# Mamba, time-warped cross-attention and 64 experts on one core: GpSimd scatters an expert's rows ahead of the gather for the expert four places on

## The reference

```
logits = einsum('te,ex->tx', x, gate)            # 4096 tokens, 64 experts
weights, selected = top_k(logits, 2); weights = softmax(weights)
sorted_x = x[token_idx]                          # 8192 rows, grouped by expert
h0, h1 = ragged_dot(sorted_x, w0), ragged_dot(sorted_x, w1)   # 256 -> 512, float32
out_sorted = ragged_dot(silu(h0) * h1, wo)                    # 512 -> 256
out[t] = sum over its 2 experts of weight * out_sorted[row]
x = x + out
```

## Time and profile before

| | |
|---|---|
| median of 3 runs | 1307.4 us (1305.8 to 1307.7) |
| the profiled execution's own time | 1307.59 us |
| its span, first to last instruction | 1305.8 us |
| mean granted TensorE clock | 0.888 |
| busy: TensorE, DVE, GpSimd, ACT | 1036.5, 927.7, 695.1, 580.2 us |
| gathers (L2221) in the profile | 93, mean 0.997 us of GpSimd |
| scatters (L2228) in the profile | 95, mean 1.575 us of GpSimd |
| the experts' stretch | about 837 to 1262 us |

### The profile page before, as it was taken

One profiled execution on the slowest core, in us unless ns is written; L12 is line 12 of the kernel. 1 busy time (PEld: TensorE's weight loads), 2 busy tenths in 40 slices (PEclk: granted clock), 3 DMA queues, 4 the chain that ended last, 5 costly groups with the idle time before them and its releaser, 6 DMA issues. The chain is left out here.

```text
span 1305.8 us, 21090 instructions
## 1 busy us (share of the span) xinstructions
PE 1036.5 (79%) x6867; PEld 924.2 (71%) x6867; DVE 927.7 (71%) x2072; ACT 580.2 (44%) x1286; POOL 695.1 (53%) x609
## 2 busy tenths in 40 slices
PE   5767888787878768477746788799999999999970
PEld 4666767686767757466511576599999999999960
DVE  6999999999999996688798599433333333333348
ACT  3768787878778764344340454121221222222210
POOL 4886868788888870200000554346556565655620
PEclk8889989999999999555578899599999999999985
DMA  8644555464646551122203244499999999999939
GB/s 241 191 142 143 162 164 176 135 203 140 190 150 199 158 168 42 26 41 49 41 1 129 89 149 151 167 291 277 267 271 281 292 288 303 295 306 298 278 105 351
DMA packets 177597, 239.82 MB, mean 184 GB/s; under 512 B 33778, under 2 KB 104486, under 8 KB 176848
## 3 DMA queue, kind: packets, MB, share of 16 engines
q1 hardware_dynamic: 153968, 215.06, 52.1%
q0 software_dynamic: 17184, 18.97, 7.0%
q10 hardware_dynamic: 6336, 4.44, 1.1%
HBM read 203.01 MB, written 31.19 MB: 179 GB/s over the span
## 5 line engine op out<-in xcount | busy, mean ns | idle before, releaser
L1010 PE MATMUL st_y_ps<-ident,st_hc 128*128 128x128 f32 x2048 | 273.6, 292 | 113.3 <-DVE st_hc L529 113.2
L1010 PEld LDWEIGHTS st_y_ps<-ident,st_hc 128*128 128x128 f32 x2048 | 255.4, 203 | 135.6 <-DVE st_hc L529 134.7
L412 POOL TENSOR_TENSOR st_u<-st_dx,codes 128x1024 f32<-128x1024 f32 x127 | 296.4, 2361 | 39.2 <-DVE st_h L521 31.4
L521 DVE TENSOR_TENSOR_SCAN st_h<-st_da,st_u 128x512 f32<-128x512 f32 x256 | 297.6, 1203 | 0.2 <-POOL st_u L412 0.2
L2288 PE MATMUL mo_h<-mo_xt,w 128*128 128x128 f32 (+17 forms) x2048 | 282.1, 289 | 2.0 <-DVE mo_xt L2411 2.0
L2288 PEld LDWEIGHTS mo_h<-mo_xt,w 128*128 128x128 f32 x2048 | 271.6, 193 | 6.6 <-issue 2.7
L2417 DVE TENSOR_TENSOR mo_inter<-mo_silu,mo_h 128x128 f32<-128x128 f32 (+17 forms) x256 | 77.8, 304 | 246.2 <-ACT mo_silu L2370 204.3
L2228 POOL DMA_INDIRECT outs<-mo_o,choice x95 | 149.6, 1575 | 149.2 <-DVE mo_o L2428 130.3
L2370 ACT ACTIVATE mo_silu<-mo_h 128x128 f32<-128x128 f32 (+17 forms) x256 | 74.4, 291 | 286.6 <-PE mo_h L2288 198.5
L748 ACT ACTIVATE st_da<-st_delta,st_a_neg 128x510 f32<-128x510 f32 x256 | 172.1, 685 | 58.6 <-DVE st_h L521 54.1
L529 DVE TENSOR_TENSOR st_hc<-st_h,st_cps 128x1024 f32<-128x1024 f32 x128 | 152.5, 1192 | 0.0
(11 more groups left out here) (394 smaller groups left out, 1472.9 us busy)
## 6 DMA issues: line engine op xcount, KB each, us to landing
codes<-bc SPq DMA_DIRECT2D x256, 256.0 KB, 3.7
w<-in_L_ffn_w_dram SPq DMA_DIRECT2D x128, 512.0 KB
wo<-in_L_ffn_wo_dram SPq DMA_DIRECT2D x64, 512.0 KB
outs<-ex_zero SPq DMA_DIRECT2D x16, 512.0 KB, 3.2
co_got<-outs SPq DMA_DIRECT2D x16, 512.0 KB, 6.0
wave<-dist SPq DMA_DIRECT2D x16, 274.0 KB
x<-in_x_dram SPq DMA_DIRECT2D x8, 512.0 KB, 9.4
st_cx<-in_ctx_dram SPq DMA_DIRECT2D x8, 512.0 KB, 4.0
```

The costliest lines, as they stand in the source:

```text
L412: nc.gpsimd.tensor_tensor(u_sb[k % URING][:, :, :], dx[p % 2][:, :, :], over_chunks(b_sb[k % BRING]), ALU.mult).then_inc(u_ok, 1)
L521: nc.vector.tensor_tensor_scan(h_sb[k % HRING][:, dh, :], da_ps[dh][:, :], u_sb[k % URING][:, dh, :], 0.0, ALU.mult, ALU.add).then_inc(h_o ...
L1010: m = nc.tensor.matmul(y_ps[t // 2][:, t % 2, dh * P:(dh + 1) * P], hc_sb[k % RING][:, dh, t * P:(t + 1) * P], K.ident[:, :], start=False, ...
```

## The change

In GpSimd's loop over places, the scatter of place k is called ahead of the gather for place k+4, and no longer behind it (and behind the copy and the late gather, at place 59).

```
             for k in range(RANKS):
+                scatter(k)
                 if k + XR < RANKS:
                     gather(k + XR)
                 if k + XR == RANKS:
...
                                                  ).then_inc(x_in[LAST], 16)
-                scatter(k)
             n = late_count(pool)
```

## The result

| | before | after |
|---|---|---|
| median | 1307.38 us (6 runs, 1305.8 to 1308.04) | 1311.51 us (6 runs, 1309.84 to 1312.11) |
| ratio | | 1.0028 (1.0018 to 1.0039) |
| the profiled execution: time, span | 1307.59, 1305.8 us | 1312.11, 1310.4 us |

What follows compares the result with a forecast made beforehand. The prediction took TensorE's matmuls to bound the experts' stretch. With nothing added and nothing exposed, it forecast an unchanged median of 1307.4 us (chance 0.82), range 1304.5 to 1311 us.

Steps and rivals of the forecast that it cites:

- What bounds the kernel: Experts' stretch, 860 to 1240 us: TensorE busy 380.00 of 380 us, so a GpSimd change can only lengthen it.
- What moves: GpSimd's queue: same instructions and durations; even gathers go out 9.1 us later, odd gathers 4.4, odd scatters 1.2.
- The even gathers' room: Last issue of an even gather to TensorE's turn: 8.7 us at place 50, smallest 8.5 at place 62; cost nothing.
- The odd scatters' 1.2 us: Odd scatters start 1.2 us later; DVE needs their output buffer four places on, so hidden, over 9 us to spare.
- The first rival, late even gathers: Even gathers land after TensorE's turn, stalling every second one, 15 stalls: 12 us slower, 1319; chance 0.11.
- small form: Late even gathers at only the crowded first few places, up to 1 us each: 1 to 5 us, 1308 to 1312.
- The second, collision with the weights: Even gathers push weight loads back on the DMA engines, 0.5 us each, 15 us if exposed 30 times: 1322; chance 0.02.
- Scatters get ahead: Results seem to leave earlier; at most place 4's gather frees the first weight loads, 2.5 us, 1305; chance 0.05.
- What would show it: Signs in the changed profile: GpSimd's new order, TensorE busy 380.0 of 380, no weight-load wait for a DMA into gathered rows.

Runs made afterwards that it cites:

- e1: The changed kernel, with each odd place's scatter also waiting for the fourth up-product of the wide place behind it: 1308.95 us, ratio 1.0007.
- e5: The kernel before in its own order, with each odd place's scatter also waiting for DVE's second product of the next wide place: 1306.62 us, ratio 0.9995.
- e9: The changed kernel with a GpSimd memset of 0.54 us behind every gather: 1307.33 us, ratio 0.9998.
- e6: The changed kernel without the weight loads of places 4 to 62, which reuse the first four places' weights: 1311.83 us, ratio 1.0040.
- e4: The kernel before with the scatter moved ahead of the gather at even places alone: 1335.76 us, ratio 1.0206.
- e8: e4 with plain scatters, which write their rows without the add: 1357.82 us, ratio 1.0385.
- e11: The kernel before, in its own order, with plain scatters that write without the add: 1332.93 us, ratio 1.0190.
- e7: e4 without the weight loads of places 4 to 62, which reuse the first four places' weights: 1326.69 us, ratio 1.0153.
- e3: The kernel before with the scatter moved ahead of the gather at odd places alone: 1307.59 us, ratio 0.9997.
- e10: e4 with a GpSimd memset of 0.54 us behind every gather: 1307.42 us, ratio 0.9997.
- e12: The kernel before with plain scatters and a GpSimd memset of 0.33 us behind every gather and scatter: 1314.15 us, ratio 1.0043.

## Why the prediction was wrong

- **What bounds the kernel** held: TensorE's matmuls, at a clock of 1.00, and no DMA that they wait for. What I took from it didn't hold: that with TensorE at 380 of 380 us there is only the DMA to ask about. ACT and DVE stand in a chain between the up-products and the down-products of the same place, and for small rooms that chain has 0.4 us of slack.
- **What moves** held to 0.1 us: two scatters, two gathers, scatter, gather. In place 58 the scatter starts 3.28 us behind the place's beginning by the forecast's pattern and 3.30 us in the trace.
- **The even gathers' room** held. No turn waited for a gather. The last one went out 8.96 us ahead of the turn of place 62, for 8.5 forecast:

```profile
1241.39 0.91 POOL L2221 DMA_INDIRECT mo_xg<-xn,table  x1 [0.30 <-issue]
...
1250.35 0.59 PE L2274 MATMUL mo_xt_ps<-ident,mo_xg 128*128 128x128 f32 x4
```

The landing time in it was too short: the trace's records of landings, incomplete as they are, have the last one of an even gather 6.1 us after its issue in the median, 7.1 at place 10 and 8.2 at place 6, where the forecast took 5.4 (place 50: 5.5). That left 2.4 us ahead of the turn at the least.

- **The step that failed** is the one on "The odd scatters' 1.2 us", answered with "Hidden, over 9 us to spare", with nothing in the sum for it. GpSimd's durations did stay the same (scatters 149.7 us in all, for 149.6), but I asked only who waits for the scatter's rows. Moved behind two gathers, it is the third indirect DMA in 2.6 us, and in that row TensorE's signal to ACT is held for 0.28 to 0.67 us in each wide place from 32 to 60: 3.8 us instead of nothing. e1 (scatter out of the row: no loss), e5 (same moment, no row: no loss) and e9 (same order, 0.5 us of pause: no loss) each take it away.
- **The first rival, late even gathers,** had the direction and, with 1308 to 1312 in its small form, the size, but not the cause: e1 has them as late, without the loss; and the wide places that lose are the last ones, not the crowded first. **The second, collision with the weights,** falls by e6. **Scatters get ahead** came to nothing: a scatter lands 6.3 us after its issue in the median where it took 7.0, and nobody waits for it.
- **What would show it** was chosen badly. "TensorE busy 380.0 of 380" is off by 0.65 us only, of 4. The count of matmuls in the window, or the length of a place from start to start, shows it all.
- The Trainium skill (DMA: Bandwidth & Descriptors, Anatomy of one DMA) calls the generation of descriptors small, and says that many can be emitted before the cost of one more shows. It says that of the time of one DMA, and gives no price for other engines. These runs show such a price for indirect DMAs of up to 128 rows, issued 1.2 to 1.4 us apart: 28, 50 and 25 us in e4, e8 and e11.

What stays open is what the 1.4 us is, and why other engines' signals stop with it: the views show no engine or queue that is busy for it. e6 says that it isn't the traffic of the weights, and that no DMA packet need be moving meanwhile; e4 beside e7 says that this traffic lengthens it.

## What to carry to other kernels

When an edit moves indirect DMAs on GpSimd, look at the spacing of their starts, and not only at when their rows land: three or more, each about 1.3 us behind the one ahead, held a hand-over from TensorE to ACT or DVE that came just behind them, and a memset of half a microsecond behind each gather took the loss away. Three in a row at another moment (e3) cost nothing, so what matters too is which hand-over falls there. Before calling a stream "hidden", find the shortest chain through other engines beside it; here it was up-product, silu, product, down-product, with 0.4 us to spare. And compare step lengths from start to start, since a busy share of 100% with modelled ends can hide a 1% loss.

## What the runs showed of the hardware

- Indirect DMAs that GpSimd issues 1.2 to 1.4 us apart can hold TensorE's completion signals to ACT and DVE. A pair held a silu by up to 0.58 us (before, place 56), three in a row by 0.28 to 0.67 (the change, places 32 to 60), four by up to 2.07 (e4), six by up to 3.78 (e8). With starts about 1.6 us apart or more no silu was held (e9, e10); at 1.4 to 1.6 some were (e12, up to 1.39).
- A faster issuer can make a slower kernel: a plain scatter keeps GpSimd 0.98 us in the mean (e8), one with an add 1.58, and the plain one cost 25 us more in the order of before, 22 more in e4's.
- The hold doesn't need busy DMA engines (e6, share 0.29, and not one packet from 1230.3 to 1231.7 around a hold of 0.70 us), but with them long runs cost more: 28 us against 19 (e4, e7). The weight loads also slow the scatters' landing: 6.3 us from issue in the median in the changed kernel, 3.9 without them (e6).
